# A gated cross-attention block: token tiles become the stationary operand of the distance products, and x is transposed before it is normalised

## What is computed

```python
D = sqrt(max(aa + bb - 2 * ctx @ layernorm(x).T, 0))       # 154 x 2048 distances
R[i, j] = D[i, j] + min(R[i-1, j], R[i, j-1], R[i-1, j-1])  # dynamic time warping, then a backtrack
expanded[j] = sum of ctx[i] over the cells (i, j) of the path
x1 = x + tanh(g_xattn) * expanded
logits = layernorm(x1) @ gate_w.T                           # 8 experts, the best 2 with softmax weights
out = x1 + tanh(g_ffn) * sum_e w_e * (layernorm(x1) @ expert_w[e].T)
```

## Time and profile before

| | us |
|---|---|
| timed runs, median of 3 (lowest, highest) | 637.68 (637.3, 638.35) |
| profiled execution: its own time, and its span | 639.95, 638.2 |
| busy in the span: PE, DVE, ACT, POOL | 490.0, 298.9, 250.3, 237.6 |
| last two matmul records of the last unit | 98.6 to 99.7 |
| first step of the wave, and end of the wave | 74.5, 170.5 |

### The profile page before, as it was taken

One profiled execution on the slowest core, in us unless ns is written; L12 is line 12 of the kernel. 1 busy time (PEld: TensorE's weight loads), 2 busy tenths in 40 slices (PEclk: granted clock), 3 DMA queues, 4 the chain that ended last, 5 costly groups with the idle time before them and its releaser, 6 DMA issues.

```text
span 638.2 us, 7598 instructions
## 1 busy us (share of the span) xinstructions
PE 490.0 (77%) x1994; PEld 256.9 (40%) x2006; DVE 298.9 (47%) x1522; ACT 250.3 (39%) x460; POOL 237.6 (37%) x229
## 2 busy tenths in 40 slices
PE   3899997667700000474999899999999999999994
PEld 3554334445400000233545454444445444444441
DVE  7788974999998887799982400000000000000000
ACT  3665477464420000087578523222223332222221
POOL 4002903000000000012343356686677666766742
PEclk9899999896655555585999999999999999999998
DMA  9912524970007000375977966787787778777864
GB/s 297 372 33 69 163 59 125 261 187 20 2 0 263 1 1 5 133 275 173 311 217 185 356 129 109 136 164 137 134 159 138 137 135 158 122 137 136 153 101 61
DMA packets 56107, 91.76 MB, mean 144 GB/s; under 512 B 19263, under 2 KB 19263, under 8 KB 55907
## 3 DMA queue, kind: packets, MB, share of 16 engines
q0 software_dynamic: 18016, 43.00, 36.0%
q1 hardware_dynamic: 33056, 39.03, 18.9%
q10 hardware_dynamic: 4995, 9.25, 4.7%
HBM read 50.05 MB, written 41.21 MB: 143 GB/s over the span
## 4 chain that ended last, share of the span: by engine, by line
PE 60%; DVE 28%; DMA 4%; issue 3%; ACT 2%; SPq 1%; POOL 0%; ACTq 0%; POOLq 0%; DVEq 0%
PE psum L1690 40%; PE psum L1463 8%; DVE met L880 5%; PE psum L1675 5%; DVE waves L803 4%; DVE tokens L883 3%; DVE tokens L818 3%; PE psum L1439 2%; DVE tokens L946 2%; DVE shf L794 2%; PE psum L1617 2%; DVE tokens L806 1%; DMA am<-in_ctx_dram 1%; DMA tokens<-x_rows,gather_ids 1%; DVE tokens L797 1%
## 5 line engine op out<-in xcount | busy, mean ns | idle before, releaser
L1690 PE MATMUL psum<-big,tokens 128*128 x624 | 282.3, 596 | 0.2 <-ACT tokens L1371 0.2
L1690 PEld LDWEIGHTS psum<-big,tokens 128*128 128x128 f32 x624 | 113.1, 191 | 114.0 <-issue 114.0
L640 POOL DMA_INDIRECT tokens<-x_rows,gather_ids x78 | 77.8, 998 | 44.8 <-issue 23.0
L653 POOL DMA_INDIRECT out_dram<-work,add_ids x40 | 65.0, 1626 | 55.8 <-DMA out_dram<-work,add_ids 19.8
L653 POOL DMA_INDIRECT out_dram<-prow,add_ids x38 | 59.9, 1576 | 46.2 <-DMA out_dram<-work,add_ids 13.4
L1381 ACT ACTIVATE work<-psum,tile_shares 128x512 f32<-128x512 f32 x40 | 27.4, 686 | 101.2 <-PE psum L1690 95.2
L660 POOL DMA_DIRECT2D out_dram<-tokens x2 | 1.8, 910 | 168.7 <-DVE tokens L946 168.7
L1381 ACT ACTIVATE prow<-psum,tile_shares 128x512 f32<-128x512 f32 x38 | 26.0, 686 | 92.1 <-PE psum L1690 92.1
L1463 PE MATMUL psum<-big,aT 128*80 128x512 f32 (+1 forms) x128 | 60.3, 602 | 0.0
L1342 ACT ACTIVATE stage<-tokens,nm 128x512 f32<-128x512 f32 x32 | 21.6, 711 | 96.6 <-DVE tokens L946 96.6
L1585 PE MATMUL psum<-side,work 128*128 128x2 f32 x8 | 1.9, 356 | 70.6 <-DVE work L905 70.6
(11 more groups left out here) (322 smaller groups left out, 625.4 us busy)
## 6 DMA issues: line engine op xcount, KB each, us to landing
tokens<-in_x_dram SPq DMA_DIRECT2D x16, 1024.0 KB, 10.9
stage<-in_L_ffn_expert_w_dram ACTq DMA_DIRECT2D x8, 1024.0 KB, 7.4
x_rows<-stage SPq DMA_DIRECT2D x32, 256.0 KB, 2.6
out_dram<-tokens SPq DMA_DIRECT2D x6, 1024.0 KB, 7.9
tokens<-dist_rows SPq DMA_DIRECT2D x52, 64.0 KB, 3.1
dist_rows<-work SPq DMA_DIRECT2D x16, 160.0 KB, 2.0
out_dram<-tokens POOLq DMA_DIRECT2D x2, 1024.0 KB, 5.2
dist_rows<-prow SPq DMA_DIRECT2D x5, 256.0 KB, 11.1
```

The costliest lines, as they stand in the source:

```text
L640: pool.indirect_dma_start(out=xin[:, n % UX, :], out_offset=None, in_=x2_d[b][:, :], in_offset=bass.IndirectOffsetOnAxis(ap=gids[:, b, j:j ...
L653: pool.indirect_dma_start(out=out_d.rearrange("b t c -> (b t) c"), in_=yout(n), in_offset=None, out_offset=bass.IndirectOffsetOnAxis(ap=ai ...
L1690: ins = nc.tensor.matmul(psum[:, UP + n % UP, :], xinT[:, n % UX, c, :], expT[:, bass.ds(own, 1), c, :].rearrange("p o d -> p (o d)"), sta ...
```

## The change

PE's roles in the distance products are swapped. x is transposed as it arrives, without the norm. `products(i)` takes one tile of 128 tokens as stationary operand (f32, 128x128) and moves the context with the 8 gate columns past it: 162 columns, 4 chunks, 4 tiles a group, 128 matmuls in all. DVE reads each 128x162 result from PSUM (`squares_by_token`), scales it by the token's 1/std and adds the token's squared norm, both of them scalars by partition now; it keeps the 8 gate columns (`xgs`). PE turns the squares back with 8 transposes a group (`turned_back`) into 80x512 units for ACT. A group now makes its two units of both halves, one after the other, so chunk 0 waits for 8 units and every other chunk for all 16.

So that the norm's mean drops out of the product, the context is centred on DVE (`ctx_centred`), its norms come from its mean and variance (`ctx_norms`), and the gate gets its mean column from there. The context's load moves from ACT's queue to the head of SP's, the identity matrix is made first on POOL, and POOL's split of the context starts as soon as its statistics are done. DVE's order is: context, stats(0), stats(1), the border memsets that came first before (`borders`), stats(2), then squares(i) and stats(i+3), with the lane constants between i = 3 and i = 4. ACT lays the first codes before the last two units, and issues expert load 0 before the last four units and load 1 behind them. The transposes of the x gate (L1551) and their scaling (L895) go.

The diff, cut to its core:

```diff
-    UNITS = [(b, g // 2, g) for g in (0, 3, 1, 2) for b in range(B)]
...
+    UNITS = [(i % B, h, ORDER[i] % GB) for i in range(NG) for h in range(2)]
@@ sync
+            sp.dma_start(am[:, :, :], ctx_d[:, 0:SM, :].rearrange("b p c -> p b c")).then_inc(s_ctx, 16)
             for g in ORDER:
                 sp.dma_start(x[:, GT * g:GT * g + GT, :], x_v[g]).then_inc(s_x[g], 16)
-                units = min(NU, 4 * (k + 1))
+                units = NU // 2 if k == 0 else NU
-            for u in range(7):
+            for u in range(NU // 2):
                 distances_out(u)
             sp.wait_ge(s_pad, 16 * (2 * B + 1))
-            sp.wait_ge(s_xn, GT * 7)
+            sp.wait_ge(s_tr, CH * (NG - 1))
+            sp.wait_ge(s_stat, GT * (NG - 1))
             chunk(0)
-            distances_out(7)
-            chunk(1)
...
+            for u in range(NU // 2, NU):
                 distances_out(u)
-            for k in range(3, NC):
+            for k in range(1, NC):
                 chunk(k)
@@ gpsimd
-            pool.wait_ge(s_tr, CH * NG)
-            pool.wait_ge(s_xn, NT)
...
+            pool.wait_ge(s_cc, 2)
+            pool.wait_ge(s_aam, 1)
@@ vector
+            def ctx_centred(r):
...
+                for b in range(B):
+                    ins = v.bn_stats(cst[0:n, r, b, :], a[:, b, :])
+                link(ins)
+                for b in range(B):
+                    ins = v.bn_aggr(cmv[0:n, r, b, :], cst[0:n, r, b, :])
+                link(ins)
+                for b in range(B):
+                    ins = v.tensor_scalar(ctxc[0:n, 2 * r + b, :], a[:, b, :], cmv[0:n, r, b, 0:1], None, ALU.subtract)
+                ins.then_inc(s_cc, 1)
+            def stats(i):
...
+                link(v.tensor_scalar(bb[:, sl], mv[:, sl, 1], EPS, None, ALU.add))
+                link(v.reciprocal(bb[:, sl], bb[:, sl]))
+                link(v.tensor_scalar(bb[:, sl], bb[:, sl], -float(C) * EPS, float(C), ALU.mult, ALU.add))
+            def squares_by_token(i):
...
+                v.wait_ge(s_std, i + 1)
+                link(v.reciprocal(rstd[:, sl], std[:, sl]))
+                if i >= 2:
+                    v.wait_ge(s_d2, 2 * (i - 1))
                 for k in range(GT):
                     t = GT * g + k
-                    v.tensor_scalar(stage[:, i % 2, k, :], x[:, t, :], mv[:, t, 0:1], rstd[:, t:t + 1],
-                                    ALU.subtract, ALU.mult).then_inc(s_xn, 1)
+                    got = psum[:, 4 + k // 2, k % 2 * SG:(k % 2 + 1) * SG]
+                    if k % 2 == 0:
+                        v.wait_ge(s_d1, GT * i + k + 2)
+                    v.tensor_scalar(sq[:, i % 2, k, :], got, rstd[:, t:t + 1], bb[:, t:t + 1],
+                                    ALU.mult, ALU.add).then_inc(s_ev, 1)
+                    if k % 2:
+                        v.tensor_copy(xgs[:, t - 1:t + 1, :],
...
+            ctx_centred(0)
+            ctx_centred(1)
+            ctx_norms()
+            for i in range(2):
+                stats(i)
+            borders()
+            stats(2)
+            for i in range(AHEADS):
+                squares_by_token(i)
+                if i + 3 < NG:
+                    stats(i + 3)
@@ scalar
-            act.dma_start(am[:, :, :], ctx_d[:, 0:SM, :].rearrange("b p c -> p b c")).then_inc(s_ctx, 16)
+            gate_centred()
             roots(0)
             for n in range(B):
                 context_turned(n)
-            for i in range(NG):
+            for c in range(CH):
+                copy(0, c)
+            for n in range(B, 2 * B):
+                context_turned(n)
+            roots(1)
+            for i in range(1, NG):
                 for c in range(CH):
                     copy(i, c)
+                if i == 1:
+                    gate_turned()
+                    context_norms_turned()
                 if i + 1 < NG:
                     roots(i + 1)
+                if i >= 2:
+                    for h in range(2):
+                        distances(2 * (i - 2) + h)
+            act.dma_start(stage[:, 0, :, :], exp_v[0]).then_inc(s_w[0], 16)
+            for u in range(NU - 4, NU):
                 distances(u)
+                if u == NU - 3:
+                    codes_laid(0)
+            act.dma_start(stage[:, 1, :, :], exp_v[1]).then_inc(s_w[1], 16)
+            for k in range(1, 4):
+                codes_laid(k)
@@ tensor
+            def products(i):
+                b, at = ORDER[i] // GB, ORDER[i] * GW
+                pe.wait_ge(s_tra, CH * (i + 1))
+                for k in range(GT):
+                    if i and k % 2 == 0:
+                        pe.wait_ge(s_ev, GT * (i - 1) + k + 2)
+                        pe.wait_ge(s_xgs, 2 * (i - 1) + k // 2 + 1)
+                    to = psum[:, 4 + k // 2, k % 2 * SG:(k % 2 + 1) * SG]
+                    for c in range(CH):
+                        ins = nc.tensor.matmul(to, xT[:, c, at + k * P:at + (k + 1) * P], aT[:, b, c, :],
+                                               start=(c == 0), stop=(c == CH - 1))
+                    ins.then_inc(s_d1, 1)
+            def turned_back(i):
+                pe.wait_ge(s_ev, GT * (i + 1))
+                for h in range(2):
+                    if i:
+                        pe.wait_ge(s_dq, 2 * (i - 1) + h + 1)
+                    for k in range(GT):
+                        ins = nc.tensor.transpose(psum[0:HP, 6 + h, k * P:(k + 1) * P], sq[:, i % 2, k, h * H:h * H + HP],
+                                                  ident[:, :])
+                    ins.then_inc(s_d2, 1)
+            for n in range(B):
+                context(n)
+            transposes(0)
+            for n in range(B, 2 * B):
+                context(n)
+            transposes(1)
+            gate()
+            context_norms()
+            pe.wait_ge(s_gwc, B + 1)
+            pe.wait_ge(s_aab, 2)
+            for i in range(NG):
+                products(i)
+                if i:
+                    turned_back(i - 1)
+                if i + 2 < NG:
+                    transposes(i + 2)
+            turned_back(NG - 1)
```

More of the change, by code:

```diff
@@ L685, in _ @@
             v.memset(eps[:, :], EPS).then_inc(s_eps, 1)
[L686 to L709, removed]
@@ L711, in stats, with borders @@
-            def stats(i, ks):
+            def borders():
+                v.memset(bigtile[:, :], BIG).then_inc(s_big, 1)
+                link(v.memset(edge, BIG))
+                for q in range(2 * B):
+                    link(v.memset(edge[q * NB:q * NB + NB - 1, :], 0.0))
+                for k in range(3):
+                    v.memset(mring[:, k, 0:1], BIG)
+                link(v.memset(rring[:, RR - 1, :], BIG))
+                link(v.tensor_scalar(rring[:, RR - 1, 0:1], edge, -1.0, BIG, ALU.mult, ALU.add))
+                link(v.memset(inner, 1.0))
+                v.memset(outer, 0.0)
+                v.memset(sign[0:P // 2, :], 1.0)
+                v.memset(sign[P // 2:P, :], -1.0)
+                v.memset(offj[0:P // 2, :], 0.0)
+                link(v.memset(offj[P // 2:P, :], float(T - 1)))
+                v.memset(side[:, :], 0.0)
+                for q in range(2 * B):
+                    v.memset(inner[q * NB:q * NB + 1, :], 0.0)
+                    link(v.memset(outer[q * NB:q * NB + 1, :], BIG))
+                for q in range(2 * B):
+                    b = q % B
+                    v.memset(side[q * NB:(q + 1) * NB, b:b + 1], 1.0)
@@ L712, in stats, with ctx_norms @@
+            def ctx_norms():
+                link(v.tensor_tensor(aa[:, :, :], cmv[:, :, :, 0], cmv[:, :, :, 0], ALU.mult))
+                link(v.tensor_tensor(aa[:, :, :], aa[:, :, :], cmv[:, :, :, 1], ALU.add))
+                v.tensor_scalar(aa[:, :, :], aa[:, :, :], float(C), None, ALU.mult).then_inc(s_aam, 1)
+            def stats(i):
                 g = ORDER[i]
+                sl = slice(GT * g, GT * g + GT)
                 v.wait_ge(s_x[g], 16)
-                for k in ks:
+                for k in range(GT):
@@ L715, in stats @@
                     ins = v.bn_stats(st6[:, GT * g + k, :], x[:, GT * g + k, :])
[L716 to L721, removed]
+                link(ins)
+                for k in range(GT):
+                    ins = v.bn_aggr(mv[:, GT * g + k, :], st6[:, GT * g + k, :])
+                    ins.then_inc(s_stat, 1)
@@ L780, in _ @@
             ins.then_inc(s_lane, 1)
+            for i in range(AHEADS, NG):
+                squares_by_token(i)
+                if i + 3 < NG:
+                    stats(i + 3)
             dedge = flat[:, dlo:dlo + DR * CS * W1].rearrange("p (n w) -> p n w", w=W1)[:, :, 0]
-            v.wait_ge(s_xn, NT)
+            v.wait_ge(s_tr, CH * NG)
             link(v.memset(dedge, 0.0))
@@ L1252, in codes_laid @@
                     s_code, 1)
-            for u in range(NG - 1, NU):
+            for u in range(NU - 4, NU):
                 distances(u)
-                if u >= NG + 1 and u < NG + 5:
```

(22 more changed lines are left out.)

234 lines of the change are left out of this document (66 added, 168 removed).

## The result

The changed kernel took 643.13 us (median of 4 runs, 642.39 to 643.86), the kernel before 637.61 beside it: ratio 1.0084, interval 1.0068 to 1.0100. Run again in five rounds it took 642.67 against 638.46: ratio 1.0061, interval 1.0043 to 1.0078. So it is some 4 us slower (5.4 and 3.9 by the two ratios), where 2.6 us faster was forecast and the range ended at 641.

What follows compares the result with a forecast made beforehand. PE's work was taken to bound stage one: the last products end 22.8 us earlier, 20.2 given back (12.1 for formerly hidden wave steps, 8.1 for a longer tail), so 637.68 - 2.6 = 635.1 us; range 629.5 to 641.

Steps and rivals of the forecast that it cites:

- The start: Stage one up to the second group's products: context load, statistics, POOL contention and border memsets put their start at 30.9 us.
- P1: PE's distance products of the second group, counting from 0; forecast to start at 30.9 us, waiting for DVE's first squares.
- Behind t: From the last group's products to the scan of step 8: 13.3 us plus 1.7 for slowed chunk 1 loads, 15.0.
- t above 80: Sign that the forecast is wrong: the last group's products end after 80 us; forecast 76.9, before the change 99.70.
- P: PE's time for one group's distance products, 32 records of 162 columns: 4.5 us.
- T and B: PE's time per group for sixteen transposes, 1.8 us, and for the 8 new transposes back, 0.9 us.
- The third rival: In PE's products the weight load sets the pace, 0.190 us a record, 6.1 us a group: 646.3 us; chance 9%.
- The price of the lost cover: In DVE's wave, 16 scan steps formerly hidden under stage one's later units now follow it: 12.1 us.
- The border memsets: On DVE behind the second group's statistics, formerly free before x arrived: 4.3 us on the way to the second products.
- The fourth rival: Behind the last products, the expert load is fully in the way of chunk 1: 2.1 us more, 637.2; chance 13%.
- The second rival: At the start, context lands at 11 to 12 or 4-wide operations wait a full POOL operation: 639.1 us; chance 15%.
- the first: Rival: 4-wide operations don't wait for POOL and chunk 1 isn't slowed, 3.6 + 1.7 us earlier: 629.8; chance 18%.

Runs made afterwards that it cites:

- Before_chunks_late: Kernel before, only the chunk order changed: chunk 0 waits for 8 units, all others for 16; 650.00 us against 638.79, ratio 1.0186.
- split_late: Changed kernel with POOL's split of the context put back behind the last transposes and statistics; 637.67 us against 638.83 for the kernel before, ratio 0.9983.
- borders_first: Changed kernel with the border memsets moved to the front of DVE's program; 641.92 us, ratio 1.0047 to the kernel before.
- five edits: Changed kernel with late split, borders first, expert loads moved, first code copy late, rest of context on SP's queue ahead of x; 634.73 us, ratio 0.9941.
- five edits to its order, load 1 held back: Changed kernel with all five order edits, expert load 1 also waiting until chunk 1 has landed; 630.86 us against 638.46 for the kernel before, ratio 0.9875.
- expert_moved: Changed kernel with expert load 0 issued in the fourth group and load 1 placed behind the code copies; 640.49 us, ratio 1.0038 to the kernel before.
- expert_clear: Changed kernel with expert load 0 in the fourth group, load 1 waiting until chunk 1 has landed; 637.43 us against 638.46 for the kernel before, ratio 0.9985.
- four edits: Changed kernel with late split, borders first, expert loads moved and first code copy late; 635.78 us, ratio 0.9959 to the kernel before.

## Why the prediction was wrong

The forecast had the wave's end at 167.9, the profile has it at 173.91. Two steps of its sum failed by size: "The start" (P1 at 35.16, not 30.9) and "Behind t" (17.6 us, not 15.0). Its own sign of being wrong, t above 80, came true with 80.75. Step by step:

1. **PE's work was right.** P is 4.5 us (P1 from 35.16 to the 39.65 of the transposes behind it, recorded as 4.65), T and B as said (1.74 and 0.88, from start to start), and from P1 to the last product 45.6 us where 45.9 was forecast. The weight load is hidden: 256 records of 162 columns with their own loads recorded at 202 ns on average follow each other by 0.14 us (4.49 for 32), and a group takes 7.1 us. The third rival is refuted.
2. **The price of the lost cover was right.** (Cover: 16 steps of the wave that ran, before, while later units were still being made.) Before_chunks_late gives 11.7 us by the trace, 12.1 was worked out. From step 8 to the wave's end 75.6 us, forecast 76.0. It alone takes back more than half of the 19 us by which t fell.
3. **"The start" was mis-sized by 4.3 us**: P1 at 35.16 and not at 30.9. It has three terms, on two paths that end together at P1. The rest of the context was taken to land at 8.5 and was used from 10.59; the aggregates of stats(0) ended at 16.33, 1.8 late. POOL's split was charged with 1.8 us per stats, half an operation for each of two tensor_scalars; after stats(0) it took 3.3 (1.71 and 1.90 less 0.17 each), 1.5 more: each began 0.2 to 0.45 us into one of POOL's operations and waited out the rest. With these two, DVE's squares were ready at 35.01, some 4.1 late. For a wait of the statistics, the reciprocal and the reads of PSUM the forecast's sum has nothing, and no row shows that; beside POOL's split the runs had them at 2.47 us for four tiles (changed kernel), 0.17 and at most 0.45 (split_late). And P0's clock was put at nothing: in the forecast's sum T2 ends at 29.0 and P1 starts at 30.9, so P0 lay beside DVE's delay only as long as it was at most 1.9 us longer, but it was 3 us longer (7.59) and began 3.1 us late, so PE ended T2 at about 35.0, together with the squares. So the clock did matter. The border memsets, the forecast's last term there, cost almost nothing by themselves, since PE was no earlier (borders_first).

   Split_late prices the whole split at 3.9 us of P1, for which the forecast had charged 3.6; so it does not by itself explain the 4.3. Without the split the forecast's sum gives P1 at 27.3, and split_late had it at 31.23, with the context used at 10.36 and a P0 of 6.34 us. With five edits, the context used at 9.39 and P0 at 4.65, it came at 27.97. How the 4.3 us divide among the three terms is not shown by a run of its own.
4. **"Behind t" was mis-sized by 2.6 us**: step 8 at t + 17.6, not t + 15.0. The contention was put on the wrong transfer. Chunk 1's loads were charged 1.7 and were not slowed; the stores of units 11 and 15, charged 1.96 by the earlier trace rows, took 5.9 and 5.7 us beside the two expert loads. The first of them is mostly hidden and holds ACT for 1.4 us, the second stands wholly on the path, 3.7. With the loads away the term is 12.8, so they cost 4.8 us where 1.7 were charged; the rest of the sum, 13.3 without them, was 0.5 too long. The fourth rival is refuted in its letter: chunk 1's loads were not slowed.

These two terms, 4.3 and 2.6, less 0.7 gained in the products and the steps, make the 6 us between the forecast's wave end and the measured one, and turned 2.6 us faster into 3.4 slower. The second rival (context late or POOL worse, 15%) had two of the three terms of the larger one; P0's clock stood in no rival. The fourth had the right cause on the wrong DMA. Of the first, the larger half is refuted, operations of 4 elements do wait; its other half, that chunk 1's loads are not slowed, came true. The two misses came together, and I had given each cause a case of its own and added none up.

The wave's end accounts for 6.0 of the 8.0 us between the forecast, 635.1, and the median, 643.13; alone it would have given 641.1, at the edge of the range. The other 2.0 come from the step from profile to median: the forecast took off 2.27, as for the kernel before, whose first profile had long expert products, and the changed kernel's profile is only 0.33 above its median. Why their length varies is open. By the repeat's medians the change costs 4.2 us, so the 5.5 of the first medians are in part chance.

With five edits to its order, load 1 held back, and none to its arithmetic, the changed kernel is 1.25% faster than the kernel before, 7.6 us.

## To carry to other kernels

When work moves to the start of a kernel, its contention can move with it, as that of POOL's split did here (1.71 and 1.90 us for 0.17): look at what the waiting instructions do from the second they are freed, engine by engine and queue by queue, and price every transfer behind an issue, the stores as well as the loads (5.9 and 5.7 us for 2.0 here). A DMA that follows a copy in an engine's program need not be behind it in time: in expert_moved it was issued at 88.09, ahead of copies that started at 88.61. If it has to stay away from a transfer, let it wait for a semaphore that is set behind that transfer, as load 1 waits for chunk 1's in expert_clear (1.97 us for the last store). And an engine's saving is worth only what the stage behind it did not already hide: here 12 of the 19 us by which t fell went for steps that had been hidden.

## What the runs showed of the hardware

- DVE tensor_scalar operations of only 4 elements a partition, SBUF to SBUF, waited for POOL's operations (up to 1.90 us for 0.17). The statistics of four tiles that ran beside POOL's operations from 20.25 on took the same 2.47 us as without them (split_late). Reciprocals of the same size and reads of PSUM were not held, as split_late shows, where POOL's split lies beside the last squares: a reciprocal took 0.17 at 72.29, and no read of 162 columns took more than 0.45.
- A 160 KB store issued 0.65 us behind a 1 MB load on another queue took 5.7 to 5.9 us for 2.0, and 64 KB loads issued 6.4 us or more behind the load's issue took 2.0.
- A pause of PE of 3.13 us before P0 went with a granted clock of 0.50 for most of P0 (26.0 to 30.0), 7.59 us for 4.65. With pauses of 0.29 us in that place P0 took 6.34 and 6.45 us in two kernels and 4.65 in a third: the pause right before it doesn't tell the clock alone. The one ahead of the transposes T1 was 4.6 us in the changed kernel, 4.2 with the split late, 3.9 with four edits and 0.6 with five. With five edits and load 1 held back the two pauses were 0.8 and 1.33 us, and P0 took 6.32. What sets it is not shown.
